# Gathered rows in eight banks, with the waits of the last banks moved to an earlier turn

## The reference

```python
e = jnp.stack([tbl_0[ids[:, 0]], ..., tbl_31[ids[:, 31]]], axis=1)   # (512, 32, 128)
dot = jnp.einsum('bnd,bmd->bnm', e, e)
z = dot[:, iu, ju]                       # upper triangle, 496 values
h = jnp.concatenate([z, dense_ctx], axis=1)                          # 512 values
h = jnp.maximum(h @ W_top1 + b_top1, 0.0)                            # 512
h = jnp.maximum(h @ W_top2 + b_top2, 0.0)                            # 256
y = h @ W_top3
```

## Time and profile before

| | us |
|---|---|
| median of 3 runs | 150.77 (150.52 to 151.89) |
| the profiled execution | 150.31 |
| its span, first to last instruction | 148.5 |
| PE busy (matmul) | 119.0 (80%) |
| DVE busy | 81.2 (55%) |
| ACT busy | 68.6 (46%) |
| POOL busy | 76.0 (51%) |

### The profile page before, as it was taken

The page is one execution under the profiler, slowest core; times in us unless marked ns, Lnnn a source line. Parts: engine busy times, 40 slices in busy tenths (PEclk is TensorE's granted clock), DMA queues, the critical chain, the costliest instruction groups (busy, mean ns, idle before and its releaser), DMA issues.

```text
span 148.5 us, 2544 instructions
## 1 busy us (share of the span) xinstructions
PE 119.0 (80%) x1008; PEld 96.8 (65%) x1008; DVE 81.2 (55%) x80; ACT 68.6 (46%) x109; POOL 76.0 (51%) x80
## 2 busy tenths in 40 slices
PE   0195998789999989769599764487499989799993
PEld 0174776476777776545488564276499979699971
DVE  1599997899999999676993000020113041313300
ACT  3359806989998974069961051012024040300032
POOL 3777885747788777848777567506301700000000
PEclk9999999999999999999779969559869999999999
DMA  2797776557647868882212112205425733042000
GB/s 64 187 338 240 283 214 194 124 160 216 206 121 176 272 226 246 233 288 53 53 35 53 53 33 57 53 2 126 114 63 130 188 99 73 4 141 71 4 0 1
DMA packets 10990, 19.29 MB, mean 130 GB/s; under 512 B 2385, under 2 KB 7377, under 8 KB 10978
## 3 DMA queue, kind: packets, MB, share of 16 engines
q1 hardware_dynamic: 8290, 14.01, 32.0%
q0 software_dynamic: 2304, 4.72, 11.6%
q10 hardware_dynamic: 384, 0.39, 0.8%
HBM read 17.02 MB, written 2.13 MB: 129 GB/s over the span
## 4 chain that ended last, share of the span: by engine, by line
PE 65%; issue 14%; DVE 12%; another core or an unknown queue 4%; ACT 2%; DMA 1%; DVEq 0%
PE two_ps L479 16%; PE two_ps L481 13%; DVE onehot L290 9%; PE two_ps L519 8%; PE two_ps L528 8%; PE free_ps L519 7%; PE turn_ps L495 5%; PE free_ps L539 3%; DVE low L275 3%; PE two_ps L539 2%; ACT emb L353 2%; PE two_ps L544 1%; DMA id_sb<-row_ids 1%; PE turn_ps L528 1%
## 5 line engine op out<-in xcount | busy, mean ns | idle before, releaser
L266 POOL DMA_INDIRECT rows<-tables,row_no x72 | 75.1, 1044 | 42.3 <-issue 19.5
L479 PE MATMUL two_ps<-onehot,high 128*128 128x512 f32 x118 | 50.7, 430 | 15.5 <-DVE low L275 6.9
L290 DVE TENSOR_TENSOR onehot<-pick_id,free_ps 128x1536 fp32r<-128x1536 int16 (+2 forms) x30 | 53.1, 1800 | 4.2 <-DMA pick_id<-pick_ids 2.1
L481 PE MATMUL two_ps<-onehot,low 128*128 128x512 f32 x118 | 48.4, 410 | 0.0
L479 PEld LDWEIGHTS two_ps<-onehot,high 128*128 128x128 f32 x118 | 23.5, 199 | 27.0 <-issue 21.1
L481 PEld LDWEIGHTS two_ps<-onehot,low 128*128 128x128 f32 x118 | 23.5, 199 | 4.4
L275 DVE TENSOR_TENSOR low<-home,high 128x1024 fp32r<-128x1024 f32 (+2 forms) x17 | 18.3, 1076 | 3.0 <-ACT high L353 1.6
L519 PE MATMUL two_ps<-emb 128*64 128x64 f32 x240 | 12.8, 263 | 7.8 <-issue 6.8
L353 ACT ACTIVATE high<-home 128x1024 fp32r<-128x1024 f32 (+2 forms) x17 | 15.8, 941 | 4.9 <-DMA home<-picked 4.2
L373 ACT ACTIVATE away<-pick_id,less_row 128x512 f16<-128x512 int16 x25 | 16.7, 715 | 1.4 <-DMA pick_id<-pick_ids 1.4
L179 DVE COPY home<-free_ps 128x512 f32<-128x512 f32 x4 | 2.8, 692 | 26.4 <-remote 24.1
(11 more groups left out here) (32 smaller groups left out, 46.4 us busy)
## 6 DMA issues: line engine op xcount, KB each, us to landing
home<-picked SPq DMA_DIRECT2D x10, 512.0 KB
home<-picked SPq DMA_DIRECT2D x3, 640.0 KB
pick_id<-pick_ids SPq DMA_DIRECT2D x14, 128.0 KB
dot_out<-home SPq DMA_DIRECT2D x14, 128.0 KB, 2.5
w_sb<-w SPq DMA_DIRECT2D x3, 512.0 KB
rows<-tables,row_no POOLq DMA_INDIRECT x72
pairs<-dot_out SPq DMA_DIRECT2D x14, 64.0 KB, 2.0
home<-picked SPq DMA_DIRECT2D x4, 128.0 KB, 3.9
```

The lines of the kernel that those rows point to most:

```text
L266: pool.indirect_dma_start(rows[:, k % ROWS_HELD, i, :], None, tables, bass.IndirectOffsetOnAxis(ap=row_no[:, c:c + 1], axis=0)).then_inc(r ...
L290: dve.tensor_tensor(onehot[:, c % HOT:c % HOT + n, :], ids, own, ALU.is_equal).then_inc(onehot_dve, n)
L479: pe.matmul(out, high[:, at, D * k:D * (k + 1)], onehot[:, c % HOT, :], start=(k == 0), stop=False)
L481: pe.matmul(out, low[:, at, D * k:D * (k + 1)], onehot[:, c % HOT, :], start=False, stop=(k == KR[t] - 1)).then_inc(picked_done, 1)
```

## The change

`rows` gets 8 slots and not 4, with one arrival semaphore for each slot, so 16 KiB of a partition and not 8 KiB. The wait of POOL before bank k is split in two. A new constant `AHEAD` = 4 keeps the old distance of the gathers to the turns, and the outer `max` is what the slots need: with 8 slots bank k must wait for turn k - 8, `turned` at k - 7, and for no less than 11 (`PICK - 3`) where the old distance would ask for more.

```diff
@@ -39,7 +39,9 @@
 TURNED = PICK - 1
-TABLES_HELD, IDS_HELD, HOT, AWAY, ROWS_HELD = 3, 4, 16, 6, 4
+TABLES_HELD, IDS_HELD, HOT, AWAY, ROWS_HELD = 3, 4, 16, 6, 8
+
+AHEAD = 4
 
@@ -259,8 +261,8 @@
             for k in range(NB):
-                if k >= ROWS_HELD:
-                    pool.wait_ge(turned, k - ROWS_HELD + 1)
+                if k >= AHEAD:
+                    pool.wait_ge(turned, min(k - AHEAD + 1, max(PICK - 3, k - ROWS_HELD + 1)))
                 for i in range(TILES[k]):
```

## The result

| | before | after |
|---|---|---|
| median on the same chip, 4 runs each | 151.33 us (150.52 to 152.08) | 159.57 us (158.68 to 159.69) |
| the profiled execution | 150.31 | 158.68 |
| its span | 148.5 | 156.9 |
| mean granted clock | 0.940 | 0.913 |

The ratio is 1.053, 95% interval 1.046 to 1.061. On this chip the change makes the kernel 5.3% slower. Lines of the changed kernel are those of before plus 2: gathers at 268, dots at 521, turns at 497, layer 1 at 530.

A forecast was written before the change was run, and what follows sets the result against it. PE's finished instructions were taken to retire slowly while POOL gathers: dots under the gathers cost 2.8 us, the earlier layer 1 of block 1 gains 0.95, so + 1.85 on 150.77 gives 152.6 us; range 149.0 to 154.4.

The forecast's parts named there:

- Step 1: ACT's copy of picks 12 and 13: without POOL's pause, dots start 0.6 us later, at 87.3 (bounds 0 and 3).
- four clearings: After four gather bursts, PE or its waiting copies were freed within 1.0 to 1.8 us of the burst's end.
- Step 2: Start of the dots: PE runs ahead 3.6 us and breaks at 90.9 with 60 records out.
- Step 3: Dots under gathers, 90.9 to 105.0: PE trickles at 3.05 records per us, 103 of 128 out by then.
- Step 4: Behind the gathers: last 25 records take 1.5 us, to 106.5; group 2 starts at 107.15 and not 100.45.
- Step 5: Dot groups 2 to 5: 8.6 us without their hole plus 0.7 for low clock, ending 116.45, 2.8 us later.
- Step 6: Stores and loads of groups 0 and 1: rows in at 116.5, layer 1 at 117.15, hidden by only 0.6 us.
- rival C: Loads of groups 0 and 1 land 2 us late, so layer 1 of blocks 0 and 1 waits: 154.5; chance 0.05.
- The gain: Last burst no longer lies over the layers, so layer 1 of block 1 starts 0.95 us earlier.
- A: Second hole, at 102.5: holes last 7 us however long POOL gathers, so faster, 146.3 to 148.5; chance 0.18.
- B: Holes move with PE's stream or deferred records are made good: no change, 150.0 to 152.0, say 150.8; chance 0.14.
- B's rule: Hole at 90.3: the skill says TensorE and ScalarE never wait for others' SBUF traffic; sum near 0, 150.8.

The follow-up runs named there:

- e1: Changed kernel with its eight slots, but every bank waits for its old turn; 149.51 us beside 149.75 of the kernel before (1.001).
- e2: Changed kernel, but banks 16 to 19 ask for up to one turn more; 155.38 us (1.043).
- e6: Changed kernel with a 512-column memset on POOL before each gather of the last four banks; 147.91 us beside 151.26 (0.978).
- b1: Changed kernel with a 128-column memset on POOL between gathers of the last four banks; 156.50 us beside 148.08 (1.057).
- e9: Changed kernel, but early banks gather as far ahead as slots allow and the last three wait for dot groups 0 to 5; 166.51 us (1.099).
- b2: Changed kernel with a 512-column memset on POOL before each gather of the last six banks; 139.98 us beside 148.08 (0.945).

## Why the prediction was right or wrong

The direction and the place were right (slower by over 1% had the chance 0.48), the size was not: + 8.4 us in the span where + 1.85 was forecast, 159.57 where the range ended at 154.4. By its own steps:

- **POOL.** 103.8 forecast, 104.83 measured: the same gathers, 1.03 later, since POOL was already that much behind before 83.
- **Step 1**, start of the dots: 87.3 forecast, 84.85 measured. The missing pause did not delay ACT's copy; it came at 83.75, 0.2 us behind the turns. I took this as a cost and it was a gain of 1.85. So the first of my four clearings, ACT's copy 1.8 us behind the burst that ended at 83.83, was no sign that the copy waited for the burst: here POOL gathers all along. Nor need the gain be the change's, for e1, which asks for the turns of before, starts its dots at 83.63. It may be the chance of one execution.
- **Step 2**, the run-ahead: 60 records and a break at 90.9 forecast, 31 records and a break at 86.0 measured. It was 66 records in the kernel before, with the dots 0.8 us behind a pause of 2.08 us; 38 in e1, 1.75 us behind one of 1.66 us; 37, 31, 31 and 28 in e2, the changed kernel, e6 and b1, with no pause just before. So 66 was the largest of six and I took it for a property of PE. That the pause made it so large is likely but not shown, since e1 with a pause got no more than e2 without.
- **Step 3 failed.** It took the rate of 3.05 records per us from bursts of 9.7 and 4.7 us, and the clearing of 1.2 us from the same and the last, and held both constant over an unbroken run of 39 us (65.57 to 104.83). Measured: 1.0 per us in the mean, 0.6 per us at its end, and 4.1 us of clearing. My bounds for the clearing, 1.0 to 1.8 us, were the spread of four short cases, and those for the rate, 2 to 3.5 per us, came from two; neither was a bound for a longer run. e9 showed the sinking of the rate apart from the dots.
- **Step 4**: 107.15 forecast for group 2, 114.19 measured, 7.04 late. Split by my own steps: the clearing gave 2.86 (4.06 in place of 1.2), the last gather's later end 1.03, and 75 records left in place of 25 gave 2.82 (4.32 us in place of 1.5; 29 of the 50 are step 2's, 21 step 3's rate); turn 14 and the gap behind it gave 0.33. The clearing is the largest term.
- **Step 5**: 9.3 forecast, 7.8 measured; no low clock in 115 to 120 (1.00). 1.5 won back.
- **Step 6**: stores to loads 5.3 us, as before. The cover of 0.6 us was gone and the wait became 0.84, because groups 2 to 5 ran faster than forecast; with 0.17 us more for the turns, layer 1 of block 0 came 7.04 - 1.5 + 0.17 + 0.84 = 6.55 after its forecast of 117.15. This is rival C's mechanism, at a small price.
- **The gain** of 0.95 from turn 18's copy was found: 9.34 late at block 0, 8.39 at block 1.

The sum closes: 1.85 + 6.55 = 8.4. Rivals A and B are out: PE did not flow before POOL's last gather, and the holes did not add up to the same. B's rule holds on two of the five chips that the experiments met; on one of these the changed kernel was run, and there the change makes no difference at all (1.000). The chips were not part of the forecast, and nothing in the one trace shown could tell that.

## What to carry to other kernels

A rate, or a time to recover, that is read at a short burst is known at that length only; before it is stretched over a longer run, look whether it changes with the length of the burst, or give the longer run a bound of its own. A wait that costs its engine nothing may be the pause on which another engine lives: here the two waits of POOL, 2 and 5 us, were worth 8 us to PE, and 0.4 us more between gathers from bank 14 on was worth 11% (b2's ratio 0.945 beside 1.053, on other runs). Where a hole has no releaser in the profile, run the kernel on more than one chip before you tune against it.

## What was not expected of the hardware, and what stays open

- On three chips the kernel before took 148.1 to 151.3 us, on two 128.8 and 128.9. No trace of it was taken on the two. The changed kernel takes the same time on one of them, and beside its trace there the kernel before loses 9.1 us in dot groups 0 and 1 (13.0 beside 3.9), 5.6 in groups 2 to 5 (13.2 beside 7.6) and 6.3 up to the last turns of the picks (83.29 beside 76.96). So most of the 20 us lies where PE is held while POOL gathers; that the 6.3 us of the picks are the hold too is not shown.
- On the three, indirect gathers of POOL issued 1.25 us apart hold PE's issue and its completions. Neither 16 us of memsets on POOL nor the same bytes loaded by SP do. Plain transfers of POOL did not in 5.2 us, which is short.
- Open is by what way. Late completions beside late issue speak for something that all finished instructions pass, but that is an argument and no test. The Trainium skill, page "NOTIFIC — the notification-queue block", section 7.1, says that this block can stall an engine when its internal queue fills. No run here tests it. Since every run with a trace was recorded in the same way, it is also open whether the recording has a part in the hold.
- Open is what sets the run-ahead and the sinking rate in numbers, and why the picks of the changed kernel go at full pace up to 84 us (PE is busy 9.23 of the 9.5 us before 83.5), though its gathers had run without a pause from 65.57. e9 agrees: its picks went on at 9.58 of 10 us, from 17 to 27 us into an unbroken run, and sank only behind that.
- Not tried: one gather instruction for several tiles of rows, and another order in which dots and gathers do not meet.
